# Unread TensorE products, two bank pairs in the last unit, and another order of statistics and ranking scores in a two-layer attention and expert kernel

## The reference, cut to what matters

```
x = x + attention0(layernorm(x))   # 16 heads of 8 channels, strictly causal, softmax of q.k * scale[h]
x = x + experts0(layernorm(x))     # 16 experts, top 4, gelu(x w1 + b1) w2 + b2
x = x + attention1(layernorm(x))   # 16 heads of 64 channels
x = x + experts1(layernorm(x))     # 8 experts, top 1
```

```
S  = max(att[:, 0], 0), zero in column 0 and on the diagonal
FF = cumsum over queries of S, shifted by one row       # the "decay"
att = att - FF
keep, in each row, the diagonal and the 101 keys of smallest FF   # T = 512: int(0.2 * 512) - 1
```

## Time and profile before

| what | us |
|---|---|
| median of 3 runs | 1027.8 |
| lowest and highest run | 1025.99, 1034.94 |
| the profiled execution | 1027.24 |
| its span | 1025.4 |
| PE busy | 899.2 |
| DVE busy | 734.7 |
| ACT busy | 644.0 |
| POOL busy | 536.9 |

### The profile page before, as it was taken

One profiled execution on the slowest core, in us unless ns is written; L12 is line 12 of the kernel. 1 busy time (PEld: TensorE's weight loads), 2 busy tenths in 40 slices (PEclk: granted clock), 3 DMA queues, 4 the chain that ended last, 5 costly groups with the idle time before them and its releaser, 6 DMA issues. The chain is left out here.

```text
span 1025.4 us, 19097 instructions
## 1 busy us (share of the span) xinstructions
PE 899.2 (88%) x6022; PEld 593.6 (58%) x6022; DVE 734.7 (72%) x2087; ACT 644.0 (63%) x1433; POOL 536.9 (52%) x664
## 2 busy tenths in 40 slices
PE   5899989998899999968999999989998987963297
PEld 2444444444678888845556666657665754553197
DVE  5676777763889999867987978787887789445032
ACT  2565656544688888834866677767777766741075
POOL 4134536342704454001667867686768768951444
PEclk9999999985999999979999999999999989985599
DMA  4000001000444445130000000000000000001883
GB/s 135 1 2 1 22 2 43 2 22 2 128 137 133 123 102 121 23 119 1 1 2 1 1 2 1 2 1 2 2 1 2 1 2 1 2 1 31 293 292 102
DMA packets 31129, 47.71 MB, mean 47 GB/s; under 512 B 3804, under 2 KB 18673, under 8 KB 30912
## 3 DMA queue, kind: packets, MB, share of 16 engines
q1 hardware_dynamic: 29104, 43.42, 14.4%
q0 software_dynamic: 1504, 3.17, 0.8%
q10 hardware_dynamic: 432, 0.01, 0.0%
HBM read 40.25 MB, written 6.79 MB: 46 GB/s over the span
## 5 line engine op out<-in xcount | busy, mean ns | idle before, releaser
L1481 POOL TENSOR_SCALAR probs<-probs,rinv 128x128 f32<-128x128 f32 (+3 forms) x256 | 274.0, 1087 | 109.8 <-DVE rinv L1349 109.8
L1343 DVE CUSTOM_DVE_ANT_0 probs<-psum,adj 128x128 f32<-128x128 f32 (+3 forms) x256 | 122.1, 477 | 58.9 <-PE psum L1208 43.1
L1416 ACT ACTIVATE probs<-probs,rowmin 128x128 f32<-128x128 f32 (+3 forms) x256 | 141.7, 559 | 29.0 <-DVE rowmin L1343 27.8
L1425 ACT ACTIVATE pt<-psum 128x128 f32<-128x128 f32 (+3 forms) x256 | 98.3, 435 | 74.9 <-PE psum L1218 73.0
L823 ACT ACTIVATE pT<-psum 128x1024 f32<-128x1024 f32 (+3 forms) x128 | 89.8, 702 | 65.1 <-PE psum L585 64.0
L1208 PE MATMUL psum<-k_sb,q_sb 64*128 64x256 f32 (+3 forms) x512 | 111.1, 487 | 21.6 <-DVE rowmin L1343 21.0
L751 DVE TENSOR_REDUCE top<-psum 128x2 f32<-128x256 f32 (+3 forms) x128 | 102.2, 817 | 20.4 <-PE psum L573 20.1
L1332 DVE MAX8 top<-w 128x8 f32<-128x131 f32 (+3 forms) x208 | 103.2, 496 | 4.6
L1789 ACT ACTIVATE r_hid<-psum,b1t 128x512 f32<-128x512 f32 x125 | 82.5, 689 | 31.6 <-PE psum L1628 28.3
L1218 PEld LDWEIGHTS psum<-ident,probs 128*128 128x128 f32 x640 | 68.3, 141 | 58.2 <-POOL probs L1481 32.7
L882 POOL TENSOR_SCALAR_AFFINE_SELECT pT<-pT 128x512 f32<-128x512 f32 x64 | 41.0, 640 | 115.1 <-ACT pT L823 115.0
(11 more groups left out here) (304 smaller groups left out, 1887.1 us busy)
## 6 DMA issues: line engine op xcount, KB each, us to landing
r_share<-shares SPq DMA_DIRECT2D x12, 1024.0 KB, 6.8
s_wb<-in_w_all SPq DMA_DIRECT2D x23, 514.5 KB
sorted_x<-blank SPq DMA_DIRECT2D x1, 2967.0 KB, 11.6
s_xg<-sorted_x SPq DMA_DIRECT2D x23, 129.0 KB, 2.9
r_w1s<-in_w SPq DMA_DIRECT2D x16, 128.0 KB, 5.7
r_w2s<-in_w SPq DMA_DIRECT2D x16, 128.0 KB, 6.1
r_share<-shares SPq DMA_DIRECT2D x6, 256.0 KB, 3.6
r_share<-shares SPq DMA_DIRECT2D x2, 768.0 KB, 5.3
```

The source lines that it names most:

```text
L1343: dve.tensor_tensor_reduce(probs[:, k, 0:K], s_bank[h][:, 0:K], adj[:, OFF[i]:OFF[i] + K], 1.0, FLOOR, ALU.add, ALU.min, rowmin[:, k:k + 1 ...
L1416: act.activation(probs[:, k, 0:K], probs[:, k, 0:K], ACT.Exp, bias=rowmin[:, k:k + 1], scale=-1.0, accum_out=rsum[:, k:k + 1]).then_inc(ex ...
L1425: act.activation(pt[:, (2 * n + h) % 4, 0:K], t_bank[h][:, 0:K], ACT.Copy).then_inc(pt_ready, 1)
L1481: pool.tensor_scalar(probs[:, k, 0:K], probs[:, k, 0:K], rinv[:, k:k + 1], None, ALU.mult).then_inc(normed, 1)
```

## The change

Four edits:

- A helper `pe_warm` issues n products of `ident` with itself into the first 128 columns of a bank. Nothing reads them. In the first attention: 8 ahead of the x fill, 2 behind the wait for the weights, 8 behind the k fill, and 2 behind every step pair from s0 = 0 to 18, all in bank 4. In the second: 12 ahead of the x fill, 6 behind it and 3 behind the k fill of pair 0, all in bank 0.
- The last unit of the first attention uses two bank pairs in turn for the shifted scores, 4 and 5 and then 2 and 3. Its second pair waits for the exp before the one it waited for until now. New waits: the first item of that unit waits until all maxima are taken, and the first expert products wait until all exps are done.
- In `FIRST`, dec of tile 0 comes between the second and the third ranking score. DVE does 3 ranking steps behind it, 3 behind the third score's drain and 20 behind the fourth's.
- `dve_stats` is parted. For tiles 4 to 15 DVE does bn_stats, then `dve_split_x`, then bn_aggr, variance and reciprocal.

```diff
+        def pe_warm(pe, bank, n):
+            for _ in range(n):
+                pe.matmul(bank[:, 0:P], ident[:], ident[:], start=True, stop=True, skip_group_check=True)
...
-                e_bank = banks[4:6]
...
+                ENDING = NS - ITEMS
+
+                def e_bank(c):
+                    return 2 if c >= ENDING and c // 2 % 2 else 4
...
+                    if c == ENDING:
+                        pe.wait_ge(reduced, NS // 2)
                     if c >= 2:
-                        pe.wait_ge(exped, c // 2)
-                    pe.matmul(e_bank[c % 2][:, 0:W], kst[rows, U % 3, kb * P:(kb + 1) * P], q2[rows, U % 2, kb * P:N],
+                        pe.wait_ge(exped, (c if c < ENDING + 2 else c - 2) // 2)
+                    pe.matmul(banks[e_bank(c) + c % 2][:, 0:W], kst[rows, U % 3, kb * P:(kb + 1) * P], q2[rows, U % 2, kb * P:N],
...
                     if f == 0:
                         pe.wait_ge(reduced, NS // 2)
+                        pe.wait_ge(exped, NS // 2)
...
                 def pe_program(pe):
+                    pe_warm(pe, banks[4], 8)
                     pe_fill(pe, ("x", 0))
                     pe.wait_ge(w_loaded[0], 64)
+                    pe_warm(pe, banks[4], 2)
                     pe_fill(pe, ("q", 0))
                     pe_fill(pe, ("k", 0))
+                    pe_warm(pe, banks[4], 8)
...
+                        if s0 + 2 < LAG:
+                            pe_warm(pe, banks[4], 2)
...
-                    act.activation(pT[:, c % PR:c % PR + 2, 0:W], psum[:, 4:6, 0:W], ACT.Exp).then_inc(exped, 1)
+                    act.activation(pT[:, c % PR:c % PR + 2, 0:W], psum[:, e_bank(c):e_bank(c) + 2, 0:W], ACT.Exp).then_inc(exped, 1)
...
-            FIRST = [("x", 0, 0), ("q", 0, 0), ("k", 0, 0)] + [("rs", 0, i) for i in range(NT)] + [("dec", 0, 0)]
+            FIRST = [("x", 0, 0), ("q", 0, 0), ("k", 0, 0), ("rs", 0, 0), ("rs", 0, 1), ("dec", 0, 0), ("rs", 0, 2), ("rs", 0, 3)]
...
+                    pe_warm(pe, s_bank[0], 12)
                     for use in FIRST:
                         pe_fill(pe, use)
+                        pe_warm(pe, s_bank[0], {("x", 0, 0): 6, ("k", 0, 0): 3}.get(use, 0))
...
                     dve_stats(dve, c, range(NT))
+                    dve_aggr(dve, c, range(NT))
                     dve_invert_root(dve, c, 0, slice(0, NT))
                     dve_norm(dve, 0)
                     dve_stats(dve, c, range(NT, T))
+                    dve_split_x(dve, FIRST[0])
+                    dve_aggr(dve, c, range(NT, T))
                     dve_invert_root(dve, c, 1, slice(NT, T))
                     c.close()
-                    dve_split_x(dve, FIRST[0])
                     for use in FIRST:
                         if use[0] in BY_DVE:
                             dve_drain(dve, use)
-                            if use == ("dec", 0, 0):
-                                for k in range(PER_TILE):
-                                    dve_rank(dve, 0, k)
+
+                            for k in {("dec", 0, 0): range(3), ("rs", 0, 2): range(3, 6),
+                                      ("rs", 0, 3): range(6, PER_TILE)}.get(use, ()):
+                                dve_rank(dve, 0, k)
```

More of the change, by code:

```diff
@@ L1254, in dve_stats, with dve_aggr @@
                 def dve_stats(dve, c, tiles):
-                    t = slice(tiles[0], tiles[-1] + 1)
                     for i in tiles:
                         c.count(dve.bn_stats(st[:, i, :], x_tok[:, i, :]).then_inc(dve_step, 1))
+                def dve_aggr(dve, c, tiles):
+                    t = slice(tiles[0], tiles[-1] + 1)
                     dve.wait_ge(dve_step, c.done())
```

## The result

The changed kernel takes 1019.76 us (median of 4 runs, 1015.63 to 1021.81) beside 1028.51 us of the kernel before in the same comparison: ratio 0.9887, interval 0.9847 to 0.9927. A second comparison of the same file gave 1018.53 (6 runs, 1013.89 to 1022.92) against 1031.23, ratio 0.9867 (0.9834 to 0.99). The ratio given is not the quotient of the two medians, which is 0.9915 in the first and 0.9877 in the second. So the changed kernel is faster by 1.1 to 1.3%, about as forecast. Its own runs differ by up to 9 us, and so do those of the kernel before (1026.32 to 1035.84 in the second comparison). One execution of the kernel before, in the comparison that `banks_only`, `order_only`, `no_second_products` and `table_and_last_unit` share, took 4224.59 us and is in none of the ratios.

The account below looks back on a forecast made before the run. PE was busiest (88%), so slow-clock stretches and last-ending waits were taken as the bound, with DVE bounding the second opening's ranking. Terms -4.9 - 2.0 - 5.5 = -12.4 from 1027.24 gave 1014.8 us; range 1010 to 1022, own range 1011 to 1018.

Parts of the forecast that it names:

- part 1: First attention: 38 unread products lift PE's clock early, shortening the opening and units 0 and 1; -4.9 us in all.
- Part 2: Last unit of the first attention: two bank pairs remove PE's idle times before exp-bound score pairs; -2.0 us (0 to -2.6).
- Part 1, opening: Start of the first attention: clock up at 12.3 us, so q fill cold and k fill warm; -0.8 us.
- Rival B: First attention's opening: transposes break the early work, so the clock rises only behind the k fill; 1016.6 us, chance 0.18.
- Part 1, units 0 and 1: First attention's first two units: faster fills at the high clock, less the products' cost; -1.6 and -2.5 us.
- Part 3: Opening of the second attention: earlier xb_lo, earlier decay product and ranking, and 21 products holding the clock; -5.5 us.
- (a): Second opening: xb_lo moves ahead of the aggregates, root and reciprocal of twelve tiles; -1.7 us.
- (b): Second opening: tile 0's decay product moves behind the second ranking score, so ranking ends sooner; -1.4 us.
- (c): Second opening: 12 + 6 + 3 products fill PE's idle time and hold the clock up; -2.4 us (0 to -2.7).
- Rival C: Second opening: the clock falls as before, while the first attention goes as forecast; 1018.6 us, chance 0.15.
- A: First attention: the products don't lift or hold the clock and only cost time; 1030.5 us, slower than before, chance 0.12.
- D: First attention, units 0 and 1: DVE and ACT bound them, swallowing the clock's gain; 1017.7 us, chance 0.1.

Follow-up runs that it names:

- banks_only: The kernel before with the two bank pairs in the last unit, and their waits, alone: 1026.29 us, ratio 0.9962.
- order_only: The kernel before with the new order of the second opening (`FIRST`, parted statistics, ranking in three groups) and no products: 1026.73 us, ratio 0.9964.
- no_second_products: The changed kernel without the 21 unread products (12 + 6 + 3) of the second opening: 1018.45 us, ratio 0.988.
- table_and_last_unit: The changed kernel with the early Exp table, one product ahead of each last-unit mask and two behind each following step pair: 1014.05 us, ratio 0.9832.
- before_early_table: The kernel before with the early one-column Exp, which loads ACT's table sooner, alone: 1028.43 us, ratio 0.9988.
- only_first_products: The kernel before with the 38 unread products of the first attention alone: 1028.33 us, ratio 0.9973.
- changed_again: The changed kernel, unaltered, run once more for its spread and a second trace: 1018.53 us, ratio 0.9867.
- no_first_products: The changed kernel without the 38 unread products of the first attention: 1018.41 us, ratio 0.9897.
- early_table: The changed kernel with a one-column Exp on ACT behind its second root, so the table loads long before the first real exp: 1015.33 us, ratio 0.9859.
- longer_products: The changed kernel with one more product ahead of each of the 20 masks of items 20 to 39: 1016.38 us, ratio 0.987.
- table_no_step_products: The changed kernel with the early Exp table and without the 20 products behind the step pairs: 1017.8 us, ratio 0.9866.
- table_and_half_as_many: The changed kernel with the early Exp table, a product before every second last-unit mask and one behind each later step pair: 1011.17 us, ratio 0.9837.

## Why the prediction was right or wrong

**The stretches that no edit touches.** Marks of all profiled executions, in us:

| kernel | k drain, unit 3 | first expert product | expert layer | opening | rest |
|---|---|---|---|---|---|
| before | 51.1 | 248.3 | 198.5 | 30.6 | 548.0 |
| before_early_table | 51.1 | 248.3 | 198.4 | 30.6 | 547.9 |
| only_first_products | 46.5 | 244.9 | 201.0 | 32.2 | 547.5 |
| banks_only | 51.0 | 241.1 | 198.5 | 32.1 | 551.5 |
| order_only | 51.0 | 248.2 | 200.1 | 27.9 | 550.4 |
| changed | 54.4 | 247.9 | 199.2 | 24.7 | 548.3 |
| changed_again | 49.3 | 245.2 | 200.7 | 24.9 | 549.1 |
| no_first_products | 50.9 | 244.0 | 198.4 | 24.7 | 548.7 |
| no_second_products | 46.6 | 241.2 | 199.0 | 26.2 | 548.9 |
| early_table | 45.9 | 239.0 | 199.3 | 24.7 | 550.6 |
| longer_products | 49.8 | 243.0 | 198.5 | 24.7 | 547.7 |
| table_no_step_products | 48.3 | 246.6 | 198.4 | 24.7 | 547.7 |
| table_and_last_unit | 45.6 | 241.6 | 199.0 | 24.7 | 550.6 |
| table_and_half_as_many | 45.5 | 236.6 | 198.8 | 24.7 | 547.7 |

The expert layer varies by 2.6 us and the rest by 4.0, with the same code in all of them. `only_first_products` is 3.4 us ahead at the first expert product and ends level with before: 2.5 us go in the expert layer and 1.6 in an opening that is before's own, where the clock was low twice instead of once. `no_first_products` reaches its first expert product 3.8 us sooner than the changed kernel's page has it, where the fall at 33 us had put unit 3 back by 3.5.

**The forecast, 1014.8 us.** Against the 1027.8 that it started from, this is a ratio of 0.987; measured were 0.9887 and 0.9867. Direction, size and range were right, and both medians are within 5 us of the number, though above the forecast's own narrow range of 1011 to 1018. The parts were less right than the sum. Taken alone they give -2.8, -3.9 and -3.7 (the last without its products), in all -10.4; with the 1.5 to 3.2 us of the 21 products it is -11.9 to -13.6, about the forecast's -12.4. The medians of the changed kernel are 8.8 and 12.7 us under those of before. In total time part 1 shows less than its 4.9 us: 2.8 alone, with an interval up to 5.5, and nothing that can be told once the other parts are in (`no_first_products`). Part 2 gave nearly twice its term. That these two nearly cancel in the sum is luck. And the totals do not decide between the two theories of the experiments: bank pairs and second opening alone fit them as well.

**Part 1, opening: -0.8 forecast, -2.1 measured.** The failed step is "I take 12.3, the middle of the k fill" for the rise of the clock. It rose at about 9 us, so that both fills were fast. Nor do the rows bear out the evidence given for it, "about 4.7 us of unbroken work" ahead of the rise at 36 us: PE was unbroken for 7.5 us there (from 28.83), and it was busy for all 5.00 us of 20 to 25 without a rise. The early rise came true; which property of the eight products brought it was not separated. Rival B, that the transposes break the run of work and the clock rises only behind the k fill, is refuted: both fills ran fast, and the transposes already in part (0.84 us). The Trainium skill ("TensorE: Matmul & The Clock Gate", section "Part 4: PE-mode transpose") denies that transposes count for the clock. That is not tested here, since the clock rose while they ran, behind eight real products.

**Part 1, units 0 and 1: -1.6 and -2.5 forecast.** With the clock up, unit 0 gave -1.1 and unit 1 -1.5 (`only_first_products`: drains 12.19, 21.78, 35.14 against 14.26, 24.95, 39.80). The step that fails is "unit 1: 14.85 to the 11.30 of the next unit, but unit 1 has the v fill, so I take 11.7". Unit 1 also has the table load, which the low clock had hidden. With the load moved away, unit 1 takes 12.28 us instead of 14.85, -2.6, the forecast's term. That is the part of the explanation that the runs show. A slip of 0.1 us stands in the opening's sum besides: it saves 0.8 and then counts 0.9.

**Part 1, the silent step.** The sum assumes that a clock once lifted stays up until 36 us, where before has it high anyway. Five profiled executions have these products and the load in front of the first exp: it stayed up in `only_first_products`, `no_second_products` and `longer_products` (which has 20 more products there), and fell in the two of the changed kernel, for 23.9 us in one and 7 in the other. The fall came each time between PE's two waits for the first exps, at 32.8 and 33.1 us; the executions whose clock held have the same waits. With the table early it did not come in any of the three that also have the step products; without them it came at 24.7 us, before the first real exp. Three of three against two of four (`longer_products` aside) does not show that the early table prevents it, and what decides between executions with the same windows stays open. Nor does this fall explain the spread of 9 us. The two profiled executions in which it lasted 23.9 and 7 us took the same time to 0.03 us; the kernel before, without any of these products, spreads as widely; and `table_and_half_as_many`, with the table early, spreads over 14 us. The mean granted clock of each execution goes roughly with its time: in `changed_again` the two fastest have 0.949 and 0.946, the slowest 0.933. So much of the spread lies in how long the clock is low somewhere in the kernel, and where is not known of executions without a profile.

**Part 2: -2.0 forecast (0 to -2.6), -3.9 alone.** Outside the bounds. The failed step is "idle times before 233.70 and 238.45 and a smaller one before the last pair go: 2.6 at most". It counted waits only and left the products at their durations. But two pairs next to each other in the queue use four row groups, and the second pair takes no time of its own: 4 products in 0.80 us, where before took 0.79 twice. The ten executions at the low clock, 23.4 against 19.5 us for the same stretch, show the size. The pairs of 512, 384 and 128 columns do this; those of 256 stand as two groups.

**Part 3: -5.5 forecast, -5.9 measured.** (a) -1.7 was 1.77. (b) and (c): `order_only` has -2.7 for (a) and (b) where the forecast had -3.1; the 21 products give the rest, 3.2 us beside it and 1.5 beside `no_second_products`, where (c) had said 2.4. The clock did fall once more, at 459 to 460 us (0.73), up to almost 463. PE is at its low level there beside DVE's ranking, which is the bound, so it cost nothing that shows: `early_table`, `no_first_products` and the changed kernel all have 24.7 us. Rival C is refuted by the windows; in total time its 2.4 us are too few to be seen.

**Rivals A and D.** A (the products don't lift the clock) is refuted by the fills of 1.02 us. D (DVE and ACT swallow the gain) gave part 1 -2 us, where the drain of unit 3 in `only_first_products` is 4.6 us ahead. It has some truth for units 0 and 1, which gave 2.6 us instead of 4.1. Of the 1.5 us that are missing, ACT's table load is 1.1, one instruction with a name that stands in the trace of before, 1.28 us at 34.19. The 0.5 of unit 0 was not looked into.

## What to carry to other kernels

Filler products lift the clock cheaply where PE stands idle anyway (here both fills of the opening from about 2 to 1 us), but the gain need not last: in total time the 38 of the first attention gave 2.8 us alone and nothing that can be told beside the other parts. Look behind the lifted stretch for the first wait that the low clock had hidden (here an activation table load of 1.28 us in front of the first exp); moving it was worth 1.1 us of that unit, and in total time nothing that is shown. Four matmuls with 32 rows of weights, from four different row groups, took no longer than two (0.80 and 0.79 us) once they stood side by side in the queue, so a second pair of banks is worth more than the waits it removes. And where the clock falls in one execution and not in the next, compare marks at fixed instructions in several profiled executions before a term of 2 or 3 us is believed: here untouched stretches alone varied by 2.6 and 4.0 us.

## What the runs showed of the hardware that was not expected

- The granted clock of the windows view can be wrong early in a run: it prints 1.00 for 20 to 25 us of before although pairs of fills take 2.05 us against 1.12 later. It prints 1.00 on both sides of the rise at 36 us, and agrees with the durations from the first fall on. In the changed kernel it prints 1.00 for 4.7 to 8.5 us too, where eight products take 3.75 us against 1.95 later.
- The same instructions with the same busy time (1.27 of 2.00 us) are followed by a fall of the clock to 0.50 in two executions and by none in two others (`only_first_products`, `no_second_products`).
- The clock rose right behind the first eight products (4.73 to 8.48 us): the four transposes behind them took 0.84 us instead of 1.11. Before, it rose at 36 us, though PE had worked, with gaps, from 8.58 on.
- Four products with 32 rows each and 512 columns, in four row groups, take 0.80 us at the low clock and 0.50 at the high one, where two took 0.79.
